# A row's tail at other steps of the next row: scatters, the norm of xn1, the expert ranks and the gate of a recurrent two-layer block

## What is computed

```python
xn = _layernorm(x)
s = _L0_attn_ref(xn, ...)      # 16 heads, top 8 of 16+512 keys, softmax
g = _silu(_L0_ffn_ref(xn, ...))  # 8 experts, top 2
x = x + s * g
xn = _layernorm(x)
s = _L1_attn_ref(xn, ...)      # one head over the channels
g = _silu(_L1_ffn_ref(xn, ...))  # 8 experts, top 2, capacity 80 slots per expert and row
return x + s * g
```

## Time and profile before

| | us |
|---|---|
| median of 3 runs | 1442.65 (1442.06 to 1442.70) |
| the profiled execution | 1442.93 |
| its span in the trace | 1441.2 |

### The profile page before, as it was taken

How to read it: one execution, slowest core, us unless ns; L and a number is a source line. 1 busy time by engine, 2 the same in 40 slices (tenths; PEclk the granted TensorE clock), 3 DMA queues, 4 the chain that set the end, 5 groups by cost and what they waited for, 6 DMA issues and landing times.

```text
span 1441.2 us, 32467 instructions
## 1 busy us (share of the span) xinstructions
PE 1344.9 (93%) x10039; PEld 1187.9 (82%) x10039; DVE 1007.4 (70%) x3163; ACT 879.5 (61%) x2257; POOL 845.3 (59%) x1675
## 2 busy tenths in 40 slices
PE   5999998998999999999999999999999999899964
PEld 4548897887899899899889988998998899788842
DVE  7817774666778677677768767776877777545765
ACT  3546775445677677677667667776767777522321
POOL 6257884443776665756656575565557576633462
PEclk9999999999999999999999999999999999999997
DMA  7017002423300000000000000000000000012231
GB/s 256 8 59 240 24 25 83 126 82 93 108 20 4 18 16 9 18 12 9 9 14 17 8 18 13 9 7 16 16 9 11 20 11 5 20 51 77 62 86 40
DMA packets 70203, 62.26 MB, mean 43 GB/s; under 512 B 10904, under 2 KB 58115, under 8 KB 70034
## 3 DMA queue, kind: packets, MB, share of 16 engines
q1 hardware_dynamic: 61842, 44.96, 10.3%
q0 software_dynamic: 8192, 15.23, 3.7%
HBM read 32.88 MB, written 25.17 MB: 40 GB/s over the span
## 4 chain that ended last, share of the span: by engine, by line
PE 79%; DVE 8%; issue 5%; POOL 4%; ACT 2%; DMA 1%; DVEq 1%; POOLq 0%; SPq 0%
PE sa L1895 17%; PE sc L1873 15%; PE mb L1902 13%; PE tr L1884 9%; PE sc L1732 4%; PE sc L1832 3%; PE mb L2113 2%; PE sc L1875 2%; DVE kept L1413 2%; PE sa L1737 1%; PE tr L1737 1%; POOL attn L799 1%; PE sc L2101 1%; POOL x_slots L770 1%; PE sc L1854 1%
## 5 line engine op out<-in xcount | busy, mean ns | idle before, releaser
L799 POOL TENSOR_SCALAR attn<-kept,rden 128x128 f32<-128x128 f32 (+3 forms) x512 | 289.4, 565 | 324.2 <-DVE rden L1417 299.1
L1406 DVE MAX8 top<-sc 128x8 f32<-128x144 f32 (+3 forms) x512 | 263.2, 514 | 221.4 <-PE sc L1875 219.4
L1873 PE MATMUL sc<-k_hl,x_hl 128*128 128x272 f32 (+3 forms) x1920 | 371.4, 313 | 3.2 <-DVE k_hl L1398 1.7
L1895 PE MATMUL sa<-wv,attnT 128*128 128x128 f32 x2560 | 370.8, 276 | 0.0
L1032 ACT ACTIVATE attnT<-tr 128x128 f32<-128x128 f32 (+3 forms) x512 | 223.2, 436 | 227.0 <-PE tr L1884 225.1
L1895 PEld LDWEIGHTS sa<-wv,attnT 128*128 128x128 f32 x2560 | 326.3, 192 | 2.0 <-issue 1.8
L1873 PEld LDWEIGHTS sc<-k_hl,x_hl 128*128 128x128 f32 x1920 | 282.0, 190 | 23.2 <-issue 13.0
L1026 ACT ACTIVATE ex<-sc,nmax 128x144 f32<-128x144 f32 (+3 forms) x512 | 276.9, 541 | 16.7
L1413 DVE SCALAR_TENSOR_TENSOR kept<-sc,top,ex 128x144 f32<-128x144 f32 (+3 forms) x512 | 284.3, 555 | 2.5 <-ACT ex L1026 0.8
L1884 PE MATMUL tr<-ident,attn 128*128 128x128 f32 x1280 | 229.5, 277 | 25.5 <-POOL attn L799 23.6
L1884 PEld LDWEIGHTS tr<-ident,attn 128*128 128x128 f32 x1280 | 138.9, 142 | 35.8 <-POOL attn L799 31.4
(11 more groups left out here) (334 smaller groups left out, 1935.8 us busy)
## 6 DMA issues: line engine op xcount, KB each, us to landing
x_slots<-sg SPq DMA_DIRECT2D x1, 4608.0 KB, 17.1
y_slots<-wv SPq DMA_DIRECT2D x18, 256.0 KB, 2.3
x_slots<-sg SPq DMA_DIRECT2D x1, 2560.0 KB, 16.5
y_pick<-x_slots SPq DMA_DIRECT2D x10, 256.0 KB, 2.8
fb<-L_ffn_b SPq DMA_DIRECT2D x2, 1024.0 KB
attn<-x_slots SPq DMA_DIRECT2D x8, 256.0 KB, 3.3
arena<-L_attn_x SPq DMA_DIRECT2D x8, 256.0 KB, 3.3
fb<-L_ffn_W SPq DMA_DIRECT2D x8, 256.0 KB, 6.3
```

The source lines that it names most:

```text
L799: pool.tensor_scalar(dst, src[:, NM:NM + P * (t + 1)], rden[:, t:t + 1], 1.0, ALU.mult, ALU.mult).then_inc(attn_ready.sem, 1)
L1406: dve.max(top8[:, t, :], src).then_inc(top_done.sem, 1)
L1873: pe.matmul(dst[:, lo:hi], x_hl[:, a, t * P:(t + 1) * P], k_hl[:, m, k, lo:hi], start=(i == 0), stop=(i == 2 and hi < w), skip_group_check ...
L1895: ins = pe.matmul(sa[:, t * C:(t + 1) * C], src[:, j * P:(j + 1) * P], wv[:, j, k, :], start=False, stop=False, skip_group_check=True)
```

## The change

Only the tables of steps are changed; no instruction is added or removed.

- `SCATTER_AT` (rows 2 to 7): from five scatters in pair 6 and three in pair 7 to two in pair 6 and six in pair 7, no two at one step.
- `GATE_AT`: the last piece of the gate (L1434) from (6, 4) to (6, 2), in rows 1 to 7.
- `DVE_TAIL` (rows 2 to 7): piece 5 from (1, 3) to (1, 6), piece 6 from (2, 0) to (2, 3), piece 7 from (2, 4) to (2, 7), piece 8 from (3, 3) to (3, 6), piece 9 stays at (3, 7), pieces 10 to 14 from (4, 0), (4, 1), (4, 2), (4, 4), (4, 6) to (4, 3), (4, 4), (4, 5), (4, 7), (5, 1).
- `DVE_TAIL1` (row 1): pieces 9 to 14 from (4, 5), (4, 7), (5, 0), (5, 1), (5, 3), (5, 5) to (4, 6), (5, 0), (5, 1), (5, 2), (5, 4), (6, 0).
- `GATE_AT0` (row 1): the first piece of row 0's gate from (1, 2) to (1, 3).
- `PICKS_ROW`, `GATHERS_ROW` and `SCATTERS_ROW1` are new names for steps that stay what they were.

```diff
-        SCATTER_AT = ((6, 2), (6, 3), (6, 5), (6, 6), (6, 7), (7, 0), (7, 2), (7, 3))
+        SCATTER_AT = ((6, 3), (6, 6), (7, 0), (7, 1), (7, 2), (7, 3), (7, 5), (7, 6))
...
-            SCATTERS_AT = {1: tuple((7, u) for u in range(UNITS))}
+            PICKS_ROW = ((5, 5), (5, 6), (5, 7), (6, 0), (6, 1))
+            GATHERS_ROW = ((1, 3), (1, 6), (2, 3), (2, 6), (3, 3), (3, 6), (4, 3), (4, 6))
+            SCATTERS_ROW1 = ((7, 0), (7, 1), (7, 2), (7, 3), (7, 4), (7, 5), (7, 6), (7, 7))
...
-                gathers_at = GATHERS0_AT.get(b, tuple((it, u) for it in (1, 2, 3, 4) for u in (3, 6)))
-                scatters_at = SCATTERS_AT.get(b, SCATTER_AT)
+                gathers_at = GATHERS0_AT.get(b, GATHERS_ROW)
+                scatters_at = SCATTERS_ROW1 if b == 1 else SCATTER_AT
...
-            GATE_AT = ((5, 2), (5, 6), (6, 4))
+            GATE_AT = ((5, 2), (5, 6), (6, 2))
...
-            DVE_TAIL = ((0, 3), (0, 5), (0, 7), (1, 0), (1, 3), (2, 0), (2, 4), (3, 3), (3, 7), (4, 0), (4, 1), (4, 2), (4, 4), (4, 6))
-            DVE_TAIL1 = ((1, 7), (2, 0), (2, 2), (2, 3), (2, 6), (3, 0), (3, 4), (4, 0), (4, 5), (4, 7), (5, 0), (5, 1), (5, 3), (5, 5))
-            GATE_AT0 = ((1, 2), (1, 4), (1, 6))
+            DVE_TAIL = ((0, 3), (0, 5), (0, 7), (1, 0), (1, 6), (2, 3), (2, 7), (3, 6), (3, 7), (4, 3), (4, 4), (4, 5), (4, 7), (5, 1))
+            DVE_TAIL1 = ((1, 7), (2, 0), (2, 2), (2, 3), (2, 6), (3, 0), (3, 4), (4, 0), (4, 6), (5, 0), (5, 1), (5, 2), (5, 4), (6, 0))
+            GATE_AT0 = ((1, 3), (1, 4), (1, 6))
```

More of the change, by code:

```diff
@@ L863, in row @@
                             root1(b)
-                        if tail and (it, u) in PICKS_AT.get(b, ((5, 5), (5, 6), (5, 7), (6, 0), (6, 1))):
+                        if tail and (it, u) in PICKS_AT.get(b, PICKS_ROW):
                             next(routing)
```

## The result

The changed kernel takes 1433.22 us (median of 6 executions, 1431.19 to 1434.24), the kernel before, run beside it, 1442.86 us (6 executions, 1442.06 to 1444.17). The ratio is 0.993, with a 95% interval of 0.992 to 0.9941: faster by 0.7%. The forecast was 1435.3 us with a range of 1433.0 to 1441.5. The direction and the main mechanism held; the time is 2.1 us lower than the forecast. The profiled execution of the changed kernel is the longest of its six, 1434.24 us with a span of 1432.5.

What follows compares the result with a forecast made beforehand. PE was taken as the bound, other engines costing time only where PE waits. Rows 2 to 6 -5.35, row 7 -1.5, row 1 -0.9 made -7.75 us, taken as -7.5: forecast 1435.3 us, range 1433.0 to 1441.5.

Steps and rivals of the forecast that it cites:

- What bounds the kernel: Whole kernel: PE is 79% of the chain, so other engines' work costs time only where PE waits for it.
- the scatters: Pair 6, rows 2 to 7: moving scatters out removes PE's waits before (6, 2) and (6, 3), gaining 1.70 us a row.
- The gate on the picks: Pair 6: the gate's piece at (6, 2) holds POOL's last small picks, cost 0.38 us a row, bounds 0 and 0.55.
- Pair 7: Six scatters in pair 7, rows 2 to 7: cost 0, up to 0.5 us a row; length unchanged at 18.35 us.
- PE's waits did not merely move to the row's end: Rival: pair 6's waits are taken up at the row's end, time 1443 us; chance 0.08.
- the rival that this could have been: Rival: POOL's backlog at (7, 5) makes the row's end slow like row 1's, 1454 us; chance 0.08.
- Piece 14 to (5, 1): Pair 5, rows 2 to 7: later `chosen` makes PE's `positions` wait, cost 0.25 us a row, bounds 0.1 and 0.4.
- the other moves in pairs 1 to 4: Rows 2 to 7: DVE pieces moved among steps with little work, sum 0, bounds -0.1 and +0.2 us a row.
- Row 1: Row 1: DVE's wait for the gate's gathers at (1, 2) goes, -0.9 us, bounds -0.4 and -1.3.
- The later ranks add a wait of 0.2: Row 1: later ranks add 0.2 us at (5, 2), the gate's move takes as much off POOL's picks, sum 0.
- Row 7: Row 7: -1.5 us in all, from -1.70, +0.38, -1.0 for the wait before (6, 7), +0.55 given back, +0.25.
- the low end: Range's lower limit, 1433.0 us: the sum with the gate's lock at 0, -7.5 - 2.3 with the median.

Runs made afterwards that it cites:

- e1: Only the SCATTER_AT table of the change, made on the kernel before, gate left at (6, 4): 1431.43 us, ratio 0.9923.
- e5: The changed kernel with the gate's last piece back at (6, 4): 1431.79 us, ratio 0.9914 to the kernel before.
- e6: The changed kernel with row 1's DVE_TAIL1 as before, GATE_AT0 left changed: 1432.58 us, ratio 0.9927 to the kernel before.
- e8: The changed kernel with all eight scatters of rows 2 to 7 in pair 7, one a step: 1443.2 us, ratio 1.0005 to the kernel before.
- e9: The changed kernel with piece 14 at (5, 2) instead of (5, 1) in rows 2 to 7: 1455.89 us, ratio 1.0084 to the kernel before.
- e4: Only row 1's two tables, DVE_TAIL1 and GATE_AT0, changed on the kernel before: 1443.1 us, ratio 1.0002.

## Why the prediction was right, and where it missed

**What bounds the kernel, and the scatters: right.** The earlier trace rows had waits of 0.80 and 0.58 before the transposes of (6, 2) and (6, 3). PE's timeline of row 4 after the change, transposes of (6, 0) to (6, 3):

```profile
835.10 0.27 PE L1886 MATMUL tr<-ident,attn 128*128 128x128 f32 x1
836.81 0.44 PE L1886 MATMUL tr<-ident,attn 128*128 128x128 f32 x2 [0.18 <-POOL attn L801]
838.46 0.50 PE L1886 MATMUL tr<-ident,attn 128*128 128x128 f32 x3
839.91 0.66 PE L1886 MATMUL tr<-ident,attn 128*128 128x128 f32 x4
```

Both are gone and a small one stands before (6, 1), as foretold. e1 shows the term by itself: 1.70 a row.

**The gate on the picks: right on average, and two-valued.** I had put 0.38, with bounds of 0 and 0.55. POOL and DVE in row 4, then in row 6:

```profile
833.50 0.25 POOL L754 TENSOR_SCALAR at<-of_pick 128x8 f32<-128x8 f32 x1
833.90 0.40 POOL L756 TENSOR_TENSOR at<-at,of_pick 128x8 f32<-128x8 f32 x1
...
833.53 0.70 DVE L1436 SCALAR_TENSOR_TENSOR sg<-sg,facc 128x512 f32<-128x512 f32 x1
...
1084.85 0.81 POOL L754 TENSOR_SCALAR at<-of_pick 128x8 f32<-128x8 f32 x1
1085.80 0.21 POOL L756 TENSOR_TENSOR at<-at,of_pick 128x8 f32<-128x8 f32 x1
...
1084.88 0.67 DVE L1436 SCALAR_TENSOR_TENSOR sg<-sg,facc 128x512 f32<-128x512 f32 x1
```

In both rows POOL's pick L754 and DVE's gate start within 0.03 us of each other. In row 4 the pick is through in its usual 0.25, the gate takes 0.70, and the next pick is held (0.40 instead of 0.20). In row 6 the gate takes its undisturbed 0.67 and L754 is held to 0.81. `attn` of (6, 0) then comes 0.22 or 0.58 later than in e5, where the gate is elsewhere, and pair 6 is 15.07 or 15.44. Rows 3, 4 and 7 went the cheap way, rows 2 and 6 the dear one; row 5 is with the dear ones, by a hold of 0.38 on a pick that starts 0.18 later. In e6 it was rows 2, 3 and 6 that were cheap, so the race has no fixed winner. The Trainium skill, page "SBUF — State Buffer", section "Who interferes with whom", says that issue order decides which of the two engines blocks. This case's trace agrees that one goes on undisturbed and the other is held, but the recorded starts don't tell which: in both rows POOL's is the earlier by 0.03 us, and in row 6 it is the one that is held. My 0.38 lies between two prices, neither of which is 0.38.

**Pair 7: right.** 18.36 against 18.35, so PE's waits did not merely move to the row's end either. e8 priced the rival that this could have been: the mechanism was real, at 1.3 us a row (2.9 where the clock fell) and not the 3.3 that row 1 suggested, and two scatters fewer in pair 7 keep the kernel clear of it. I had taken the rival's price from row 1, whose waits at (7, 1) and (7, 2) the other rows don't have.

**The step that failed most: `positions`, the +0.25 in "Piece 14 to (5, 1)", 1.5 us over six rows.** DVE and PE in row 4 after the change:

```profile
818.10 0.18 DVE L1515 TENSOR_SCALAR chosen<-rank 128x32 bf16<-128x32 f32 x1
...
818.42 0.17 PE L1965 MATMUL tr<-chosen,before 128*128 128x8 bf16 x1
```

`chosen` ends at 818.28, 0.14 ahead of `positions`; there is no wait: in all six rows `positions` starts 4.04 us after the pair, as in the kernel before. I had counted from the reciprocal of (5, 0) at 822.59, but this row of before was an exception. DVE's timeline of the kernel before, `top` of (5, 0) and of (5, 1), in row 4 and in row 3:

```profile
819.27 0.32 DVE L1406 MAX8 top<-sc 128x8 f32<-128x144 f32 x1 [1.66 <-PE sc L1875]
...
821.23 0.45 DVE L1406 MAX8 top<-sc 128x8 f32<-128x272 f32 x1 [0.77 <-PE sc L1875]
...
691.94 0.32 DVE L1406 MAX8 top<-sc 128x8 f32<-128x144 f32 x1 [1.02 <-PE sc L1875]
...
693.55 0.45 DVE L1406 MAX8 top<-sc 128x8 f32<-128x272 f32 x1 [0.42 <-PE sc L1875]
```

From one `top` to the next it is 1.96 in row 4 and 1.61 in row 3; rows 2, 5, 6 and 7 have 1.61 too, and after the change so has row 4. (Why DVE starts 0.35 later there, with PE's own instructions as far apart as in row 3, stays open.) With 0.35 less the same sum gives `chosen` 0.1 ahead of PE, which is what came: right working on one unlike row. e9 shows how near this was to the edge. There PE does wait for `chosen`, which ends at 830.77, and starts `positions` at 830.91, the same 0.14 later. So 0.14 is what the handover takes, for which my sum had 0.04, and `chosen` came just in time, with nothing to spare. One step later the same piece costs 3.9 us a row, and over six rows that is the 23 us between e9 and the changed kernel.

**Pair 1, costed at nothing: -1.0.** The step "the other moves in pairs 1 to 4" named DVE's wait for `root` at (1, 3) and gave it no price, because PE's large waits were elsewhere. It was 0.45 us in row 4 and 0.28 in rows 2, 3 and 6 (none in row 5), and pair 1 got shorter by 0.37 in row 4 and by 0.21, 0.19 and 0.21 in those. Row 7 had no such wait and gained nothing. DVE's lead at that step is too small to hide a wait of this length. What misled me is that such a loss need not show as idle time of PE: row 3's pair 1 in the kernel before was 0.19 longer than now, and PE is busy in all of it.

```profile
630.45:645.08 14.63, 14.63 (x122) 13.69 (x122) 12.28 (x45) 10.60 (x29) 9.87 (x23) 1.00 0.08 25
```

The rest of that step, 0 in pairs 2 to 4, held.

**Row 1: the sign was right, most of the size was eaten.** Its first half came as said: pair 1 from 17.98 to 17.20. What failed is "The later ranks add a wait of 0.2 ...: 0". That wait came, as 0.35, but a larger one came with it, for which the sum had nothing. ACT and PE at row 1's (6, 1) and (6, 2) after the change:

```profile
451.44 0.20 ACT L1026 ACTIVATE nmax<-top 128x1 f32<-128x1 f32 x1 [0.38 <-DVE top L1408]
...
452.78 0.59 ACT L1034 ACTIVATE attnT<-tr 128x512 f32<-128x512 f32 x1
...
453.42 0.18 PE L1965 MATMUL tr<-chosen,before 128*128 128x8 bf16 x1 [0.71 <-ACT attnT L1034]
```

Piece 14 at (6, 0) makes `top` of (6, 1) late, ACT waits 0.38 for it, and the copy of the transposed weights of (5, 7) stands behind that in ACT's order. So PE, which has long had `chosen`, waits 0.71 for a copy; in the kernel before it waited 0.23 there. I had followed the moved piece to its reader on PE and not to what stands behind its neighbours on ACT. e4 and e6 confirm the place: pair 6 is 15.55 with the new ranks and 14.81 with the old ones, all else equal; pairs 5 and 6 together differ by 0.58.

**Row 7: -1.9 instead of -1.5.** The `positions` term (0.25) did not come and the gate took the cheap price (0.22 instead of 0.38). The wait before (6, 7) went, and the end gave back about as much as said: pair 7 fell by 0.35 where I had 0.45.

**Together.** The rows came out 1.7 us below the sum of -7.75: `positions` 1.5 and pair 1 1.0 below it, row 7's other terms 0.15, less 0.1 for the gate in rows 2 to 6 and 0.8 for row 1. I had taken 7.5 of the 7.75, so they lie 2.0 below the forecast, as the medians do (1433.2 against 1435.3). I had allowed for margins that would not hold. The larger error had the other sign: a cost that was not there and a gain that I had left out. That the time still came out inside the range is partly luck: row 1 fell 0.8 short for a reason that the prediction didn't have, and without that it would have been some 0.6 below the low end.

## What to carry to other kernels

A term that rests on a margin of one or two tenths has to be read in every row that repeats it, since the one row at hand may be the exception. A moved piece has to be followed on its own engine to the step's neighbours and from them through the order of the next engine (here DVE to ACT to PE), not only to its own reader. When one part of a change frees an engine, parts that paid before may cost afterwards (the gate: 0.2 gained alone, 0.4 lost beside the scatters), so it pays to undo the parts one by one at the end: two of five tables here were worth undoing.

## What the runs showed of the hardware

A wait of PE can cost more than its length. Six waits of 2.3 us in e9 were each followed by 3.4 us at the 1.2 GHz level, which added 1.6 us each; two waits of 1.0 and 0.8 us close together did the same at the ends of rows 4 and 6 of e8, and not at those of rows 2, 3 and 5 with the same waits. The waits of 1.0 and 0.7 at row 1's end are in all eleven profiled executions, and the level fell behind them in one, e5 (a granted clock of 0.50 from 487.1 to 490.4). The waits of 0.8 and 0.6 of the kernel before did it in none of its six rows.

When DVE's two-input operation on 512 elements and a small POOL operation start within 0.03 us of each other, the outcome differs from row to row, and the loser is held for up to 0.57 us (L754: 0.81 instead of 0.24).
